# Grouping pairs per TensorE visit in a graph layer: sums with the one-hots as weights, a broadcast through DRAM, ten looked-up batches in thirty groups

## The reference

```
msg  = relu(x[src] + edge_attr @ We + be)            # 200000 x 128
aggr = segment_sum(msg, dst, num_segments=6250)
h = (1 + eps) * x + aggr
h = relu(h @ W1 + b1) @ W2 + b2
h = (h - mean(h, 0)) * rsqrt(var(h, 0) + 1e-5) * gamma + beta
out = layernorm(x + relu(h) + x)                     # over the 128 features
```

## Time and profile before

| | |
|---|---|
| three runs | 1674.07, 1677.64, 1679.46 us |
| profiled execution, span from first to last instruction | 1673.3 us |
| PE busy, PEld busy | 1566.0 us (94%), 1221.0 us (73%) |
| DVE, ACT, POOL busy | 1234.1, 729.9, 1207.5 us |
| L507 gathers from xb | x1187, mean 970 ns |
| DMA | 151 MB, mean 90 GB/s |

### The profile page before, as it was taken

One profiled execution on the slowest core, in us unless ns is written; L12 is line 12 of the kernel. 1 busy time (PEld: TensorE's weight loads), 2 busy tenths in 40 slices (PEclk: granted clock), 3 DMA queues, 4 the chain that ended last, 5 costly groups with the idle time before them and its releaser, 6 DMA issues. The chain is left out here.

```text
span 1673.3 us, 59216 instructions
## 1 busy us (share of the span) xinstructions
PE 1566.0 (94%) x21182; PEld 1221.0 (73%) x21182; DVE 1234.1 (74%) x3384; ACT 729.9 (44%) x1479; POOL 1207.5 (72%) x1244
## 2 busy tenths in 40 slices
PE   1289999999999999999999999999999999999984
PEld 1167777777777777777777777777777777777754
DVE  2787777777777777777777777777777777777555
ACT  0244444444444444444444444444444444444445
POOL 7377777777777777777777777777777777777732
PEclk9999999999999999999999999999999999999996
DMA  9633333333433333333333333333443333333422
GB/s 242 127 71 86 86 84 84 84 84 91 92 83 83 84 84 85 83 83 85 92 90 84 82 84 83 82 84 82 93 90 84 82 84 83 83 83 84 117 88 78
DMA packets 134449, 151.00 MB, mean 90 GB/s; under 512 B 45041, under 2 KB 114352, under 8 KB 134160
## 3 DMA queue, kind: packets, MB, share of 16 engines
q0 software_dynamic: 39360, 80.66, 19.4%
q1 hardware_dynamic: 87093, 60.01, 17.1%
q10 hardware_dynamic: 7963, 9.90, 2.1%
HBM read 144.07 MB, written 6.40 MB: 90 GB/s over the span
## 5 line engine op out<-in xcount | busy, mean ns | idle before, releaser
L507 POOL DMA_INDIRECT xg<-xb,idxb x1187 | 1150.9, 970 | 397.2 <-issue 326.6
L656 ACT ACTIVATE msg<-msg 128x512 f32<-128x512 f32 x390 | 245.5, 629 | 611.4 <-DVE msg L839 567.1
L1159 PE MATMUL ps<-hot,msg 128*128 128x64 f32 x3126 | 439.2, 284 | 34.6 <-ACT msg L656 18.9
L1159 PEld LDWEIGHTS ps<-hot,msg 128*128 128x128 f32 x3126 | 387.2, 194 | 88.1 <-ACT msg L656 22.7
L625 ACT ACTIVATE iota_all<-ps 128x384 bf16<-128x384 f32 x777 | 340.3, 488 | 178.6 <-PE ps L1221 173.3
L839 DVE TENSOR_TENSOR msg<-ps,xg 128x512 f32<-128x512 f32 x390 | 268.4, 688 | 91.3 <-PE ps L1154 87.4
L1240 PEld LDWEIGHTS ps<-iota_all 128*128 128x128 bf16 x4662 | 264.4, 98 | 70.6 <-issue 70.6
L1154 PE MATMUL ps<-we,ea 64*128 64x128 f32 x3126 | 285.5, 302 | 30.7 <-DVE msg L843 26.9
L1240 PE MATMUL ps<-iota_all 128*128 128x128 bf16 x4662 | 304.8, 219 | 0.0
L826 DVE TENSOR_TENSOR hot<-rel,iota 128x256 f32<-128x256 f32 x390 | 165.1, 423 | 176.0 <-PE ps L1159 127.9
L1154 PEld LDWEIGHTS ps<-we,ea 64*128 64x128 f32 x3126 | 209.4, 190 | 71.7 <-DVE msg L843 28.0
(11 more groups left out here) (134 smaller groups left out, 957.1 us busy)
## 6 DMA issues: line engine op xcount, KB each, us to landing
ea<-in_eat SPq DMA_DIRECT2D x156, 320.0 KB
xg<-xb,idxb POOLq DMA_INDIRECT x1187
accT<-in_xt ACTq DMA_DIRECT2D x1, 3125.0 KB
x<-in_xt ACTq DMA_DIRECT2D x1, 3125.0 KB
iota_all<-in_x ACTq DMA_DIRECT2D x1, 3080.0 KB, 38.7
out<-iota_all SPq DMA_DIRECT2D x5, 512.0 KB
xb<-iota_all SPq DMA_DIRECT2D x3, 784.0 KB, 5.8
idxb<-in_src_loop SPq DMA_DIRECT2D x78, 10.0 KB
```

What stands on the lines that cost most here:

```text
L507: pool.indirect_dma_start(out=xg[0:rows, slot, j, :], out_offset=None, in_=of, in_offset=bass.IndirectOffsetOnAxis(ap=index, axis=0)).then ...
L656: act.activation(msg[:, k, :, :], msg[:, k, :, :], ACT.Relu).then_inc(s_msg, 1)
L1159: last = pe.matmul(ps_win(), msg[0:r, k, j, :], hot[0:r, k, j, :], start=(m == 0), stop=(m == len(tiles) - 1))
```

## The change: what it does

- **Pairs.** A step of every engine is now two groups. ITERS is 13 (SPANS = 6 spans of 5 groups, ROUND = 30 groups, STEPS = 15); iteration 0 and the last are written out. TensorE does both linears (8 matmuls), then the window of the pair before.
- **Window.** `hot` (128x64) is the weight, in two column tiles (group 0 of the pair in columns 0 to 63, group 1 in 64 to 127), and `msg` (128 columns) streams. The result is 128 nodes by 128 features; ScalarE copies it to `winS`, TensorE transposes it (`turn`), and VectorE adds both halves to `accT`. `msg` and `hot` have three buffers (TURN) of a pair each; `one_hot` is one instruction of 512 columns.
- **Batches.** 10 in 30 groups (every third group, `SORTED`), live from batch 4 of iteration 0 to batch 5 of iteration 12: 122 batches, 366 tiles. There are 30 visits in 30 groups, each with 2 or 3 picks and joins (`SHARE`). Two sets of `sel1` and `sel2`, three PSUM banks.
- **Lows.** `spread_lows` on DVE and `share_lows` on PE are gone. ScalarE copies the lows to `lowS` (float16), SP stores them to DRAM and loads them back with a broadcast to `lowB` (128x896). `sel1` is made from that by two instructions that compare with a number per partition.
- **Rest.** The gather ring is 15 groups; groups 0 to 13 are gathered from x, and all four bias additions (`lift`) stand together. The twelve early chunks stand in steps 10 to 13 of the last iteration, three in each, the twelfth's second product in step 14. The doubling of `xT` (ACT L674) goes to GpSimd, behind its last gather.

The core of the diff:

```diff
-    SORTED = (3, 6, 9)
-    STEPS = (((0, 1), ()), ((2, 3), ()), ((4, 5), ()), ((6, 7), ()), ((8, 9), ()), ((10, 11), ()),
...
+    SORTED = (2, 5, 8, 11, 14, 17, 20, 23, 26, 29)
+    FIRST = tuple(3 * k - 3 for k in range(NB))
+    SHARE = tuple((3, 2, 2) if k % 2 else (2, 3, 2) for k in range(NB))
+    K0 = 4
+    K1 = 5
+    UNBIASED = 14
+    BANKS = (3, 7, 4)
...
+            def spread_lows(j, k):
+                b = batch(j, k)
+                wait_apart(sp, s_low, b + 1)
+                if not isinstance(b, int) or b:
+                    wait_apart(sp, s_lowB, 16 * b)
+                sp.dma_start(lowD.rearrange("o (b r) -> (o b) r", r=CAP), lowS[:, :]).then_inc(s_lowD, 16)
+                if not isinstance(b, int) or b:
+                    wait_apart(sp, s_sel1, b)
+                wait_apart(sp, s_lowD, 16 * (b + 1))
+                sp.dma_start(lowB[:, :], lowD.partition_broadcast(P)).then_inc(s_lowB, 16)
...
+            pool.wait_ge(s_xt, 32)
+            pool.tensor_scalar(xT, xT, 2.0, None, ALU.mult).then_inc(s_x2, 1)
...
+                act.activation(lowS[:, :], low_at, ACT.Copy).then_inc(s_low, 1)
+                if not isinstance(b, int) or b:
+                    act.wait_ge(s_sel2, b)
+                act.activation(slotS[:, :], slot_at, ACT.Copy).then_inc(s_slotS, 1)
...
-                dve.tensor_tensor(lows[:, :, :], low_at.unsqueeze(1).to_broadcast([NPAIR, NPAIR, CAP]),
-                                  ident[0:NPAIR, 0:NPAIR].unsqueeze(2).to_broadcast([NPAIR, NPAIR, CAP]), ALU.mult)\
...
+                dve.wait_ge(s_lowB, 16 * (b + 1))
+                if old is not None:
+                    dve.wait_ge(s_st1, old * NTILE + NTILE)
+                for u in range(2):
+                    last = dve.tensor_scalar(sel1[set_of(k)][:, u, :, :].rearrange("p b r -> p (b r)"), lowB[:, :],
+                                             nodeu[:, u:u + 1], None, ALU.is_equal)
...
-                    last = pe.matmul(ps_win(), msg[0:r, k, j, :], hot[0:r, k, j, :],
-                                     start=(m == 0), stop=(m == len(tiles) - 1))
...
+                pe.wait_ge(s_msg, 2 * pair + 2)
+                pe.wait_ge(s_hot, pair + 1)
+                if not isinstance(pair, int) or pair:
+                    pe.wait_ge(s_winS, pair)
+                    pe.wait_ge(s_acc, 2 * pair)
+                for j in range(GROUP):
+                    for half in range(2):
+                        last = pe.matmul(ps_win[half * WIN:(half + 1) * WIN, :], hot[:, q % TURN, half * GROUP + j, :],
+                                         msg[:, q % TURN, half * GROUP + j, :], start=(j == 0), stop=(j == GROUP - 1))
...
+                pe.wait_ge(s_winS, pair + 1)
+                pe.transpose(ps_turned, winS[:, :], ident[:, :]).then_inc(s_turned, 1)
...
+                    if not head or q:
+                        window((q - 1) % STEPS, pair - 1)
+                    for j, k, t in visit(i, 2 * q):
+                        pick(j, k, t)
+                    for j, k in phase(i, q, 2):
+                        place(j, k)
+                    for j, k, t in visit(i, 2 * q - 1):
+                        join(j, k, t)
+                    if not head or q:
+                        turn(pair - 1)
```

More of the change, by code:

```diff
@@ L635, in keep, with take @@
[L635 to L643 removed]
+            def take(j, k):
+                act.wait_ge(s_join, at_step(j, k, NTILE - 1) + 1)
+                act.activation(xg[:, SORTED[k] % RING, GROUP - HALF:GROUP, :], found, ACT.Copy).then_inc(s_took, 1)
@@ L908, in select, with select_edges @@
+            def select_edges(j, k):
+                b, old = batch(j, k), prior(j, k)
+                dve.wait_ge(s_slotS, b + 1)
+                if old is not None:
+                    dve.wait_ge(s_join, old * NTILE + NTILE)
+                for t in range(NTILE):
+                    last = dve.tensor_scalar(sel2[set_of(k)][:, t, :], slotS[:, :], nodes[:, t:t + 1], None, ALU.is_equal)
                 last.then_inc(s_sel2, 1)
@@ new lines, in iteration @@
+            def iteration(i):
+                head = isinstance(i, int) and i == 0
+                for q in range(STEPS):
+                    pair, n = i * STEPS + q, i * ROUND + 2 * q
+                    if q % 5 == 0:
+                        skip = 2 if head and q == 0 else 0
+                        _, base_of = nc.values_load_multi_w_load_instructions(
+                            basei[0:1, bass.ds(n - 2 + skip, 10 - skip)], engines=[mybir.EngineType.DVE],
+                            min_val=0, max_val=N - 1,
+                            skip_runtime_bounds_check_because="each is the least dst of a group, a row of out")
+                    for j, k in phase(i, q, 2):
+                        ranks(j, k)
+                    add_x(i, 2 * q, n)
+                    for j, k in phase(i, q, 1):
+                        select_nodes(j, k)
+                    add_x(i, 2 * q + 1, n + 1)
+                    one_hot(i, q, pair)
+                    for c in early(i, q):
+                        dve.wait_ge(s_m1[0], c + 1)
+                    if not head or q:
+                        if head and q == 1:
+                            dve.wait_ge(s_init, 2)
+                        dve.wait_ge(s_turned, pair)
+                        for half in range(2):
+                            add_window(n - 2 + half, half, base_of[2 * (q % 5) + half - skip])
+                    for j, k in phase(i, q, 1):
+                        select_edges(j, k)
+                    for j, k in phase(i, q, 3):
+                        pairs_of(j, k)
+                    if head:
+                        if q == 0:
```

672 lines of the change are left out of this document (310 added, 362 removed).

## The result

The changed kernel takes **1729.07 us** (median of 4 runs, 1723.35 to 1736.62), the one before, run beside it, 1675.97: a ratio of 1.0304 [1.0286, 1.0323], so 3% slower. The forecast was 1601, and 1652 was the upper end of the range. The profiled execution has a span of 1721.5 us.

What follows compares the result with a forecast made beforehand. TensorE bounds, GpSimd hardly behind. Per 30 groups 109.7 us of work plus 4.9 of waits is 114.6 (GpSimd 114.7); span 1673.3 - 67 - 9 = 1597, plus 4: 1601 us. Forecast 1585 to 1625, wider range 1573 to 1652.

Steps and rivals of the forecast that it cites:

- what TensorE's own work costs: TensorE per 30 groups: linears 18.8 us, windows 1.15 and transposes 0.2 per pair, batches 70.7; 109.7 in sum.
- Rival C: Window: float32 column tiles do not overlap; gain gone from 1.57 us per window, 1720 us at 1.8; chance 0.07.
- GpSimd's floor: Gathers from xb start at 84.5 us, the last at 1538; with the tail behind it, about 1580 us of span.
- rival D: Gathers slow from 1.274 to 1.32 us beside VectorE's 16-bit instructions and the broadcasts: 1637 us; chance 0.07.
- the waits, 4.9 us per 30 groups: TensorE's waits in the loop: 3.0 us for ScalarE, 1.3 for count, 0.6 for the lows, on top of 109.7.
- ScalarE's queue behind `sel2`: keep_slots and both clips wait for sel2 in five of 15 steps, delaying TensorE's window: 0.6 us x 5 = 3.0.
- rival A: New hand-offs: lows or ScalarE's queue hold TensorE a microsecond more per batch, 1620 to 1670 us; chance 0.16.
- The lows through DRAM: Two DMA hops and issues, about 5 us, fit in 6; cost 0 to 3 us a batch, 0.6 taken per 30 groups.
- `count` behind `pairs_of`: TensorE's count at a step's end waits for VectorE's last instruction in five steps: 0.25 x 5 = 1.3 us.
- The doubling: Doubling xT on GpSimd behind its last gather may take twice ScalarE's 5.40 us and cost at most 2.

Runs made afterwards that it cites:

- the looped version: Changed kernel with two slotS buffers, the lows' DMAs before edge loads, pairs_of before the sums, xT doubling on ScalarE, 30-group loop kept: 1600.59 us.
- the last version: The looped version with pairs_of moved back to the step's end, behind the sums: 1658.21 us (1636.57 to 1672.17).

## Why the prediction was wrong

**Right: what TensorE's own work costs.** Linears 1.09 us (forecast 1.25), window 1.02 (1.15), a step of 6.57 where nothing waits. In the looped version three steps of 7.25, 6.95 and 6.57 us stand for the kinds that take turns (the first two from its timeline, below), so 5 x 20.8 = 103.9 us per 30 groups, 5.8 under the forecast of 109.7. Rival C fell: the column tiles of float32 do overlap (1.02 us for 16 passes, against the 1.8 that it gave for streaming in sequence).

```profile
990.51 1.16 PE L1215 MATMUL ps<-we,ea 64*128 64x128 f32 x16
...
997.76 1.16 PE L1215 MATMUL ps<-we,ea 64*128 64x128 f32 x16
...
1004.71 1.16 PE L1215 MATMUL ps<-we,ea 64*128 64x128 f32 x16
```

**Nearly right: GpSimd's floor.** The forecast put the last gather at 1538 and 42 us behind it, a floor of 1580. In the looped version the first gather from xb starts at 88.31 (forecast 84.5), the last at 1554.63, 1.286 us apiece (forecast 1.274; rival D's 1.32 didn't come), and the span ends 41.8 later, at 1596.4, 16 above the forecast floor.

**Luck: 1600.6 against 1601.** The looped version needed four further edits, and the sum that led to 1601 doesn't describe it. That sum went by TensorE, with 109.7 of work and 4.9 of waits; the work is 103.9, the waits are larger, and GpSimd, which was put 16 us lower, sets the pace. The errors cancel.

**Wrong: the waits, 4.9 us per 30 groups.** Measured are 126.0 - 103.9 = 22.1 in the changed kernel: 16.5 of standing (126.04 - 109.49) and 5.6 that are left for half clock (2.8 of it behind the return, and 0.65 in the window at 868.73, which takes 1.67 to the next start instead of 1.02). This is the step that failed, and it is far more than the 5.8 by which TensorE's work was overestimated. By terms:

- *The loop's return* stood nowhere in the sum. It is worth 8 us for each of ten returns in the changed kernel, and 9.8 in the kernel before with a long body. Without the returns the changed kernel takes 1648.73 us, faster than before: this term alone turns the forecast gain into a loss. The instruction queue gave it away only in a profile of after, but the count was to be had before: an iteration now issues 1805 matmuls with as many weight loads. The Trainium skill (Runtime: NRT & Kernel Launch, Instruction fetch mechanics) states that a taken branch whose target is outside the window at hand forces a fetch before execution goes on. The runs agree: TensorE stands at the return of a long body (46.0 us in 10 times), and not with a short body or with no branch (0.5 us in all in the kernel before). It is a rule that spoke against this change and was missed.
- *ScalarE's queue behind `sel2`*, forecast at 3.0 us. TensorE's waits for the clip are (122.5 - 14.2) / 12.2 = 8.9. The arithmetic of the step was right (9.1 against 8.9, so nearly late), but it stood on a VectorE that is never late. In the step from 803.58 the clips end 9.6 us behind its start (813.22), 8.2 without the 1.41 us for `lowB`, and 4.49 us for `lowB` ahead of `sel1` (862.65) pass almost undiminished through the addition, `sel2`, `slotS` and both clips to TensorE. At 868.73 the wait of 3.44 us is followed by a window of 1.74 and picks at half speed. This is rival A, and its price (1620 to 1670) held for what it named: without the loop's returns the time is 1648.73.
- *The lows through DRAM*, forecast at 0.6. VectorE waits 144.8 us for them in 81 times, 1.2 for each of 122 batches; the bounds of 0 to 3 us a batch held, the 0.06 taken from between them didn't. Their place in SyncE's queue alone moved 62 us. From the store's issue to that of the load are 3.1 us at 800.87 and 5.3 at 853.60, and to the start of `sel1` 6.3 and 9.0, where "about 5" was put for the whole way. Nor was there room for 6 us: VectorE was ready for `sel1` at 805.77, 4.9 us behind the store at 800.87, as TensorE's steps are shorter than the 7.65 they were taken for.
- *`count` behind `pairs_of`*, forecast at 1.3: (49.3 - 7.3) / 12.2 = 3.4.
- *The doubling*, "at most 2": 16 where GpSimd bounds, and 10.5 alone, which is not clear of the noise. It was scaled from ScalarE (twice 5.40) and measured three times 5.40; that VectorE would stand beside it was not thought of.

**Why the parts don't add up.** Alone they give 80, 79, 62 and 10.5 us back, 231 in all; together 128. Both engines have a need per 30 groups, and the larger one counts. GpSimd's is 115. TensorE's is 103.9 and what it waits, estimated from the rows above: with the return (8) and `oh` (85.0 / 12.2 = 7.0) 118.9, above 115, so `pairs_of` pays (3.9 x 12.2 = 48 us, against 36 to 52 measured); with the return and 37.3 / 12.2 = 3.1 it is 115.0, and with `oh` alone (101.2 / 12.2 = 8.3) 112.2, both inside, so the return or the wait is free. The prediction saw the two stages balanced, 114.6 against 114.7 with TensorE's waits counted in. TensorE's work alone left 11 us of room for waits under GpSimd's 115, and 22 came.

**Open.** How much of each wait is its own and how much the half clock that it brings was not separated, and these sums of terms are estimates. That the fetch is what "issue" stands for rests on the stops coming only where a long body, a branch and instruction traffic meet; the fetch itself was not timed. Why the executions of the last version lie 36 us apart is open.

## What to carry to other kernels

Before a loop's body is made longer, count the instructions that it holds on the busiest engine, and look at the instruction queue's row: in a kernel with a loop, traffic that grows tenfold went with a stop at each return and often a clock drop behind it (8 to 10 us here). Without a loop the same traffic cost nothing. When a new single buffer is released by the last consumer of a step, everything queued behind its writer inherits each delay upstream of that consumer; a second buffer was worth 79 us. And value a fix at the balance point: the same move was worth some 50 us or nothing, depending on whether the other waits had already used up the slack against GpSimd.

## What the hardware showed that was not expected

- A return of a long loop body costs TensorE 4.6 us of standing on average in the changed kernel (46.0 in ten, 4.8 at the longest) and 2.8 us at half clock behind the one at 815.20. GpSimd, whose part of the body is 90 gathers, stood in the looped version never longer than 0.3 us for "issue" before a gather.
- A multiplication of 128x6250 float32 by a constant takes GpSimd 16.07 us (ScalarE 5.40), and a 1x1 instruction of VectorE beside it 8.39 instead of 0.15.
- Sixteen float32 passes of 128 columns over two column tiles take 1.02 us, 0.064 each, less than the 0.081 of the passes of 64 rows from which the forecast's upper value was taken.
